# Chunk 0's two norms inside the setup block, a transfer of their own for their modulation rows, and x loaded ahead of W_dt

## The reference, cut to what matters

```python
x = L0_attn_x                                         # 4 x 2048 x 256
mod = (silu(L0_c) @ L0_wmod).reshape(4, 6, 1, -1)     # layer 1 has its own c and wmod
sa, ca, ga, sb, cb, gb = mod[:, 0], ..., mod[:, 5]
ga = (2 * (ga >= 0) - 1) * maximum(abs(ga), 0.25)     # gb too
h = layernorm(x) * (1 + ca) + sa                      # first norm, then modulation
# inside the attention of layer 0:
xn = (h - mean(h)) / sqrt(var(h) + 1e-5) * norm_w + norm_b      # second norm
z, gate = xn @ W_in, silu(xn @ W_gate)
dt = clip(softplus(z @ W_dt + b_dt), 0.001, 1.0)
B, C = z @ W_B, z @ W_C
state = exp(dt * A) * state + dt * B * z              # scan over the tokens, 16 states
y = (sum over the states of state * C) * gate
x = x + ga * (h + y @ W_out)
```

## Time and profile before

| | us |
|---|---|
| median of 3 runs | 3286.13 |
| the three runs | 3277.07, 3286.13, 3286.29 |
| span of the profiled execution | 3287.9 |
| setup block, to DVE's last operation | 44.4 |
| second block's first operation, to chunk 0's first product from `xnl` on PE | 44.9 to 70.1 |
| chunk 0's first POOL product for the scans | 94.6 |
| busy: PE, DVE, ACT, POOL | 88%, 83%, 64%, 59% |

### The profile page before, as it was taken

One profiled execution on the slowest core, in us unless ns is written; L12 is line 12 of the kernel. 1 busy time (PEld: TensorE's weight loads), 2 busy tenths in 40 slices (PEclk: granted clock), 3 DMA queues, 4 the chain that ended last, 5 costly groups with the idle time before them and its releaser, 6 DMA issues.

```text
span 3287.9 us, 45422 instructions
## 1 busy us (share of the span) xinstructions
PE 2907.9 (88%) x14848; PEld 2380.8 (72%) x14848; DVE 2739.3 (83%) x4612; ACT 2096.2 (64%) x3852; POOL 1925.7 (59%) x1541
## 2 busy tenths in 40 slices
PE   6567698998999899898989989899999989998898
PEld 4455477787877778687777868777777877777676
DVE  3777989797998979799898979889897989989541
ACT  2546476676757677675767767576766767575433
POOL 1766667564766757475675756576575647666110
PEclk8558699999999999999999999999999999999998
DMA  4241123231322323232322323232232323223122
GB/s 130 96 159 39 52 81 111 92 102 64 129 82 91 125 78 100 70 118 85 100 103 81 106 79 125 66 106 92 87 109 86 108 76 121 78 71 120 56 103 76
DMA packets 152778, 308.56 MB, mean 94 GB/s; under 512 B 18368, under 2 KB 96984, under 8 KB 135136
## 3 DMA queue, kind: packets, MB, share of 16 engines
q1 hardware_dynamic: 152000, 302.52, 27.6%
q10 hardware_dynamic: 272, 1.57, 0.1%
q0 software_dynamic: 272, 1.57, 0.1%
HBM read 288.27 MB, written 17.35 MB: 93 GB/s over the span
## 4 chain that ended last, share of the span: by engine, by line
PE 48%; DVE 18%; issue 13%; ACT 12%; POOL 5%; DMA 1%; DVEq 0%; SPq 0%; POOLq 0%; ACTq 0%
PE ps_B L1870 11%; PE ps_B L1765 10%; PE ps_A L1765 8%; DVE hs L1527 8%; PE ps_H L1760 7%; DVE acc L1491 5%; PE ps_H L1778 4%; PE ps_B L1760 3%; POOL bu L1100 3%; PE ps_B L1778 3%; PE ps_B L1917 2%; ACT ps_A L1288 2%; DMA bb<-b_rows 1%; DVE hA L1719 1%; ACT acc L1300 1%
## 5 line engine op out<-in xcount | busy, mean ns | idle before, releaser
L1100 POOL TENSOR_TENSOR bu<-z,bb 128x512 f32<-128x512 f32 x1024 | 1294.2, 1290 | 289.9 <-DVE hs L1527 146.7
L1527 DVE TENSOR_TENSOR_SCAN hs<-ps_A,state,bu 128x512 f32<-128x512 f32 x768 | 976.5, 1276 | 21.7 <-ACT ps_A L1288 11.4
L1288 ACT ACTIVATE ps_A<-dt,a_neg 128x512 f32<-128x512 f32 x1024 | 699.3, 686 | 355.7 <-DVE hs L1527 351.5
L1760 PE MATMUL ps_H<-ident,hs 128*128 128x128 f32 x4096 | 652.6, 294 | 195.3 <-DVE acc L1491 123.1
L1760 PEld LDWEIGHTS ps_H<-ident,hs 128*128 128x128 f32 x4096 | 528.3, 151 | 329.2 <-DVE acc L1491 152.0
L1870 PE MATMUL ps_B<-ws_out,hid 128*128 128x256 f32 x2944 | 699.4, 382 | 15.5 <-ACT hid L1437 6.1
L1491 DVE SCALAR_TENSOR_TENSOR acc<-ps_H,ctok,acc 128x512 f32<-128x512 f32 x960 | 700.2, 731 | 8.0 <-PE ps_H L1760 7.1
L1870 PEld LDWEIGHTS ps_B<-ws_out,hid 128*128 128x128 f32 x2944 | 537.0, 191 | 85.1 <-ACT hid L1437 9.9
L1765 PE MATMUL ps_B<-fh,ws_in 128*128 128x512 f32 x1440 | 537.6, 418 | 10.3 <-DVE bl L1680 4.3
L1527 DVE TENSOR_TENSOR_SCAN hs<-ps_A,bu 128x512 f32<-128x512 f32 x256 | 310.9, 1216 | 32.2 <-ACT ps_A L1288 20.0
L1765 PEld LDWEIGHTS ps_B<-fh,ws_in 128*128 128x128 f32 x1440 | 271.0, 188 | 70.5 <-DVE cb L1664 8.1
(11 more groups left out here) (349 smaller groups left out, 4807.7 us busy)
## 6 DMA issues: line engine op xcount, KB each, us to landing
ws_in<-w_split SPq DMA_DIRECT2D x126, 1024.0 KB, 5.4
bb<-b_rows SPq DMA_DIRECT2D x256, 256.0 KB, 3.9
ws_out<-in_L_ffn_V_rwkv SPq DMA_DIRECT2D x64, 512.0 KB, 5.8
ws_out<-in_L_ffn_W SPq DMA_DIRECT2D x32, 512.0 KB, 6.9
xb<-in_L_attn_x SPq DMA_DIRECT2D x16, 512.0 KB, 5.3
n<-in_L_attn_x SPq DMA_DIRECT2D x16, 512.0 KB, 3.9
w_split<-wsp SPq DMA_DIRECT2D x8, 1024.0 KB, 5.6
out<-xb SPq DMA_DIRECT2D x16, 512.0 KB, 3.2
```

What stands on the lines that cost most here:

```text
L1100: pool.tensor_tensor(bu[:, u % 4, :], z[:, d, :], bb[:, s % 2, :], ALU.mult)\
L1288: act.activation(b.t[:, :], dt[:, d, :], ACT.Exp, scale=a_neg[:, d, s:s + 1])\
L1527: dve.tensor_tensor_scan(hs[:, s % 2, d, :], b.t[:, :], bu[:, k % 4, :], state[:, s, d:d + 1] if i % CPB else 0.0, ALU.mult, ALU.add)\
L1760: return pe.transpose(dst, src, ident[:, :])
```

## The change

- `front_norms_act` and `front_norms_pool` are the norms' code of before, now functions that both blocks use. Chunk 0's two norms are written in the setup block, behind what ACT and POOL have there; ACT's Exp of `a_neg` goes ahead of the second norm, POOL's issue of `wm1` ahead of the modulation. The other 15 chunks are as before.
- DVE signals `u_rows_s` when the rows `sA0`, `cA0`, `gA0` stand. SP then stores these three, waits, and broadcasts them as `mod_s`, still in the setup block; the other two rows are stored when `u_rows` comes.
- SP loads chunk 0 of x between W_gate and W_dt rather than behind W_B.

```diff
+                elif (layer, part) == (0, 0):
+                    dve.tensor_copy(goal, ga).then_inc(u_rows_s, 1)
...
                 for n in range(2):
+                    if n == 1:
+                        sp.dma_start(xb[0][:, :, :], x_v[0:1].rearrange("a p t m -> p (a t) m")).then_inc(s_xin.sem, 16)
                     for at, m, src in pieces[n]:
...
-                sp.dma_start(xb[0][:, :, :], x_v[0:1].rearrange("a p t m -> p (a t) m")).then_inc(s_xin.sem, 16)
...
+                front = MOD_PARTS["s"][1] * C
+                sp.wait_ge(u_rows_s, 1)
+                sp.dma_start(mods[:, 0:front], modrow[0][:, 0:front]).then_inc(u_mods, 16)
+                sp.wait_ge(u_mods, 16)
+                load_mod(sp, "s", 0)
                 sp.wait_ge(u_rows, 1)
-                sp.dma_start(mods[:, 0:LAYER_ROWS[0] * C], modrow[0][:, 0:LAYER_ROWS[0] * C]).then_inc(u_mods, 16)
-                sp.wait_ge(u_mods, 16)
+                sp.dma_start(mods[:, front:LAYER_ROWS[0] * C], modrow[0][:, front:LAYER_ROWS[0] * C]).then_inc(u_mods, 16)
+                sp.wait_ge(u_mods, 32)
...
-                pool.wait_ge(u_mm, 3)
-                pool.dma_start(wm[1][:, :, :], kp(w["L1_wmod"])).then_inc(u_wm[1], 16)
+                for name in front_norms_pool(pool, 0):
+                    if name == "h0":
+                        pool.wait_ge(u_mm, 3)
+                        pool.dma_start(wm[1][:, :, :], kp(w["L1_wmod"])).then_inc(u_wm[1], 16)
...
-                act.wait_ge(u_load, n_small)
-                act.activation(a_neg[:, :, :], a_neg[:, :, :], ACT.Exp).then_inc(u_exp, 1)
+                for name in front_norms_act(act, 0):
+                    if name == "sum1":
+                        act.wait_ge(u_load, n_small)
+                        act.activation(a_neg[:, :, :], a_neg[:, :, :], ACT.Exp).then_inc(u_exp, 1)
...
                     yield "mod_s"
-                    if i % CPB == 0:
+                    if i and i % CPB == 0:
```

More of the change, by code:

```diff
@@ L562, in build @@
         u_rows = sem("u_rows")
+        u_rows_s = sem("u_rows_s")
         u_zero = sem("u_zero")
@@ new lines, in apply, with front_norms_act @@
+        def apply(act, dst, src, rs, nb, sig):
+            for t in range(NT):
+                ins = act.activation(dst[:, t, :], src[:, t, :], ACT.Identity, scale=rs[:, t:t + 1], bias=nb[:, t:t + 1])
+            ins.then_inc(sig.sem, 1)
+        def front_norms_act(act, i):
+            x = xb[i % NX]
+            for n, (ready, at) in enumerate(((s_xin, 16), (s_h0, 1))):
+                yield f"sum{n}"
+                if n == 0:
+                    since(act, s_xg, i)
+                act.wait_ge(ready.sem, ready.at(i, at))
+                for t in range(NT):
+                    ins = act.activation(n0[:, t, :], x[:, t, :], ACT.Identity, accum_out=sum_s[:, t:t + 1])
+                ins.then_inc(s_sum.sem, 1)
+                yield f"sq{n}"
+                act.wait_ge(s_nm.sem, s_nm.at(i, n + 1))
+                for t in range(NT):
+                    ins = act.activation(n0[:, t, :], x[:, t, :], ACT.Square, bias=nm_s[:, t:t + 1],
+                                         accum_out=sq_s[:, t:t + 1])
+                ins.then_inc(s_sq.sem, 1)
+                yield f"norm{n}"
+                act.wait_ge(s_rs.sem, s_rs.at(i, n + 1))
+                apply(act, (x, n0)[n], x, rs_s, nb_s, (s_norm, s_n)[n])
@@ new lines, in front_norms_pool @@
+        def front_norms_pool(pool, i):
+            own = Own(pool, o_pool_n, i)
+            x = xb[i % NX]
+            for n in range(2):
+                yield f"mean{n}"
+                pool.wait_ge(s_sum.sem, s_sum.at(i, n + 1))
+                pool.tensor_scalar(nm_s[:, :], sum_s[:, :], -1.0 / C, None, ALU.mult).then_inc(s_nm.sem, 1)
+                yield f"rstd{n}"
+                pool.wait_ge(s_sq.sem, s_sq.at(i, n + 1))
+                own.step(pool.tensor_scalar(rs_s[:, :], sq_s[:, :], 1.0 / C, EPS, ALU.mult, ALU.add))
+                own.step(pool.tensor_tensor(rs_s[:, :], rs_s[:, :], mhalf[:, :], ALU.pow))
+                pool.tensor_tensor(nb_s[:, :], nm_s[:, :], rs_s[:, :], ALU.mult).then_inc(s_rs.sem, 1)
+                if n == 0:
+                    yield "h0"
+                    mod_ready(pool, "s", i)
+                    pool.wait_ge(s_norm.sem, s_norm.at(i, 1))
+                    own.step(pool.tensor_tensor(x[:, :, :], x[:, :, :], per_tile(m_row("cA0")), ALU.mult))
+                    pool.tensor_tensor(x[:, :, :], x[:, :, :], per_tile(m_row("sA0")), ALU.add)\
+                        .then_inc(s_h0.sem, 1)
+            own.end()
@@ L909, in since_x1 @@
                 used(eng, i - 1, "wo1")
[L911 to L920, removed]
         with nc.Block() as block:
@@ L931, in load_b @@
                       .then_inc(s_bb[s % 2].sem, 16)
[L933 to L938, removed]
-                                 mods[b:b + 1, lo * C:hi * C].to_broadcast([P, (hi - lo) * C]))\
-                      .then_inc(s_mod[part].sem, 16)
                 def step(i, name, k):
@@ L1113, in n_stream @@
                 def n_stream(i):
[L1114 removed]
                     x = xb[i % NX]
[L1116 to L1132 removed]
+                    if i:
+                        yield from front_norms_pool(pool, i)
                     yield "gx"
@@ L1206, in _ @@
             def _(act):
[L1207 to L1232 removed]
+                def n_stream(i):
+                    if i:
+                        yield from front_norms_act(act, i)
                     for c in range(KC):
```

75 lines of the change are left out of this document (25 added, 50 removed).

## The result

The changed kernel takes 3292.36 us (median of 13 runs, 3287.04 to 3295.00) against 3285.09 us of the kernel before (median of 13, 3277.07 to 3292.34). The ratio is 1.0020, 95% interval 1.0011 to 1.0028: 3.6 to 9.2 us slower, 6.7 by the means. Timed again in a later set, against 29 runs of the kernel before, the ratio was 1.0014 (1.0006 to 1.0023), 5.2 us by the means. The change does what it says, 21 us of norms leave the second block, and the kernel is slower by a fifth of a per cent or a little less. The prediction had 3288.5, 2.4 us more than before, and called that no measurable change.

A forecast was written before the change was run, and what follows sets the result against it. Norms lead the front, a chain from Ws/W2 loads through layer 1's rows just under them. Block 6.9 later, less 1.8 for loads, less 2.7 slack: +2.4 us, 3286.13 + 2.4 = 3288.5, range 3277 to 3296.

The forecast's parts named there:

- x ahead of W_dt: Setup block: 512 KB more ahead of `norm_b` in SP's queue shift its chain by 1.5 us; early first norm worth nothing.
- The rows' trip: Setup block, rows through DRAM: store 1.9 us and broadcast 4.4 after 32.3, so rows in SBUF at 38.6.
- The rival on `wm1`: Second rival, setup block: rows' store lands only behind `wm1`, broadcast takes 6.8; +8.1 us, 3294.2; 8 in 100.
- To the end of the second norm: Setup block, from POOL's multiply: 12.7 us instead of 13.5, so the second norm ends at 51.3.
- The reading with the Trainium skill: Second norm: two-input VectorE instructions contend with GpSimd reading SBUF, explaining 0.8 us; with another cause the end is 52.1.
- The border: Between setup and second block: 0.5 us, so the second block begins at 51.8 rather than 44.9, 6.9 later.
- The loads: Start of second block: Ws and W2 take 4.4 us instead of 5.8, so PE starts on Ws at 56.2.
- The rest: Second block: 14.6 us from PE's start to DVE's last row operation, 1.6 from `xnl` to PE's product; front 2.4 later.
- nothing takes the norms' place: First rival, second block: 21.6 us of norms go, 6.9 of setup growth comes back; -14.7, 3271.4; 3 in 100.
- the second chain: Start of second block: loads, Ws transposes, layer 1's rows on PE and DVE, then `xnl`; 2.7 us slack under the norms.
- PE at half clock for 17 us: Third rival, first products to end of z: idle PE leaves its clock down; +19 us, 3305; 3 in 100.
- The fall of the median to the low run: Fourth rival, whole kernel: median falls to the run 9.1 us below it; 3277.07 + 2.4 = 3279.5; 18 in 100.

The follow-up runs named there:

- its rows late: Kernel before with only DVE's rows of layer 1 put behind `xnl` (due 5 in place of -27): 0.9999 (0.9991 to 1.0008), -1.2 us.
- x load back: Changed kernel with the load of x at its old place behind W_B: 1.0005 (0.9997 to 1.0014), +2.2 us against the kernel before.
- x alone: Kernel before with only the load of x moved ahead of W_dt: 1.0008 (0.9999 to 1.0017), +2.6 us.
- the four kernels above: Changed kernel (1.0020), and it with x loaded behind W_B (1.0005), `wm1` issued before the rows (1.0016), or all five rows in one store (1.0019).
- the kernel in which the second chain was moved away, all three edits: Changed kernel with Ws/W2 loads, PE's Ws transposes and layer-1 rows in the setup block, DVE's layer-1 rows behind `xnl`: 0.9953, -15.5 us against before.
- all three and x back: Changed kernel with loads and PE's layer-1 work in setup, DVE's rows behind `xnl`, x loaded behind W_B: 0.9947, -17.2 us against before.
- all three and `wm1` early: Changed kernel with loads and PE's layer-1 work in setup, DVE's rows behind `xnl`, `wm1` issued at about 20: 0.9955, -16.0 us against before.

## Why the prediction was right

It was right in its time (3292.36 lies in 3277 to 3296, within 0.3% of before) and in its mechanism: the norms' gain whole, and given back by a block that starts later. The size is less good than that sounds. The front moved by 3.0 us for a forecast of 2.4, but the times differ by 6.7 and 5.2 in the mean, more than twice the forecast, and the range was wide enough to hold that. Step by step, forecast and measured:

1. *x ahead of W_dt.* L786's counterpart at 14.7, measured 14.51: 1.3 us where 1.5 were taken. The eighth row operation ends at 32.78 (32.50 + 0.28) for 32.3, because PE's layer-0 rows took 7.58 where they had taken 6.94; that 0.6 was in no term. It is not the change's doing: in the kernel before with its rows late, whose setup block is untouched, they took 7.58 too. The x load back and x alone show 1.36 us for this step in either direction, and that the early first norm buys nothing.

2. *The rows' trip.* 38.6 forecast, 39.64 measured. This is the term that was mis-sized, twice and in opposite directions: the store took 3.3 instead of 1.9, and the broadcast's landing 3.4 instead of 4.4. That the trip came out within half a microsecond is luck. The rival on `wm1` was partly true: it had `wm1` land at 35.6 (36.1 measured) and the store behind it. What it got wrong is the price. It added the store's whole 1.9 to the landing, while the store's trip runs beside the transfer and only its end waits (broadcast at 36.11, not 37.5), and it gave the broadcast 6.8, which took 3.4. The trip as a whole took 6.8 us for 6.3 (32.81 to 39.64), not 12. The argument against the rival, that 20 KB share sixteen engines with a transfer on another queue, does not hold, and this store has 12 KB, not 20: the four kernels above show that it lands when `wm1` has.

3. *To the end of the second norm.* 12.7 forecast, 39.64 to 52.35 is 12.7. POOL's four short operations took the 1.67 of the first norm again, not 2.50; the window of the changed kernel over the second norm shows DVE with 0.64 us of work in it:

```profile
45.00:51.00 6.00, 0.00 (x0) 0.00 (x0) 0.64 (x4) 3.93 (x16) 1.67 (x4) 0.50 0.00 0
```

The reading with the Trainium skill ("SBUF — State Buffer", section "Who interferes with whom") gave 51.3 from these terms and 52.1 without it. The stretch itself has decided for the shorter one. The kernel before with its rows late shows the cause apart: with DVE's rows taken away and nothing else changed, the four operations took 1.66 us for 2.50. The kernel with x alone ahead agrees with the Trainium skill's condition of two inputs. There two of the four ran, but for 0.09 us, beside DVE operations with one input (L666, L672 and L673) and took 0.23 and 0.20 us, as with DVE idle; the other two ran for the most part beside operations with two inputs (L676, L678 and L679) and took 0.35 and 1.21.

4. *The border.* 0.5 forecast, 0.27 measured (52.35 to 52.62). The second block began at 52.62 for 51.8: the rows were 1.0 late after steps 1 and 2, and 0.2 came back here.

5. *The loads.* 4.4 forecast, 4.3 measured (52.62 to 56.92). The loads moved into the setup block show what their place behind the border costs as a whole: 4.75 us at the first product.

6. *The rest.* 14.6 forecast from PE's start to DVE's last row operation, 14.7 measured (56.92 to 71.66); `xnl` to PE's first product 1.4 for 1.6. The front ended 3.0 us later where 2.4 were forecast.

That DVE's rows, not something else, held `xnl`, was read from 2.7 us of slack in a timeline. It stood the strongest test here: one number in DVE's table, no work removed, gave 6.6 us at the first product in the changed kernel and 0.85 in the kernel before, and the 0.85 has a cause of its own.

**The rivals.** That nothing takes the norms' place was wrong as it stood (-14.7), but its figure is close to that of the kernel in which the second chain was moved away: -15.5. PE at half clock for 17 us did not come: the first products ran at 0.50 and the clock rose some 4 us after the first of them, as in the kernel before, only 3 us later:

```profile
74.00:76.00 2.00, 2.00 (x6) 1.54 (x5) 1.49 (x4) 0.00 (x0) 0.00 (x0) 0.50 0.00 0
76.00:80.00 4.00, 4.00 (x16) 3.17 (x16) 0.43 (x1) 1.95 (x3) 0.00 (x0) 0.85 0.12 39
```

The fall of the median to the low run did not come either. One sum of the chances is off: half of the second rival, the third and the rest are 9 in 100, not 8.

**What stays open.** The profiled executions are 2.7 us apart, the means of the runs 6.7 and 5.2. The second interval (2.0 to 7.6) holds the front's 3.7, the first (3.6 to 9.2) ends above the front's 2.9. The profiled execution of before took longer than that kernel's mean (span 3287.9 and, as in the changed kernel, 1.8 around it: 3289.7, for a mean of 3285), which hides some 4 us in that pair. Between POOL's first product of chunk 1 and the end of the span, single executions take 3015 to 3029 us, and the two of the changed kernel 3025.0 and 3029.2, with the same program. Whether some 2 us more are due to the change, behind the front, no run here decides.

## What to carry to other kernels

Before work is moved ahead of a block's border, list what is issued first behind that border (here two loads) and follow those to the end: a gain on one chain is worth no more than the slack of the chain just under it, less the delay of the border. The chain of waits shows only the longest; the idle time in front of a joining operation (2.71 us at `xnl`) shows how far the next one is below. And where an order is written down as numbers, an order that was free under the old bound (DVE's rows ahead of `xnl`) has to be set anew once the bound has moved.

## What the runs showed of the hardware

**Beside DVE's rows POOL's small operations take longer.** Four of them on 128x4 took 2.50 us, and 1.66 with the rows moved away; on a chain of waits that 0.84 us was found whole at the next engine's first product.

**A small store can wait for a large load of another queue.** From its issue to the next one, 12 KB took 1.6 us with `wm1` landed before (two kernels), and 20 KB, issued as `wm1` landed, 1.9. With the 1.5 MB in flight on POOL's queue 12 KB took 3.1 to 3.3 in eight profiled executions, and in each the next issue came within 0.2 us of `wm1`'s landing. It is not so for any large transfer: with `wm1` issued before the rows, SP's second store (8 KB, issued at 35.73) had landed by 37.3, while the 384 KB broadcast ahead of it on the same queue landed at 38.3.

**PE's clock at the first product.** In the changed kernel PE is idle 7.7 us ahead of it and its products take 0.76 and 0.63 us (granted 0.50, the 1.2 GHz level); with the rows behind `xnl`, and with all three edits, it had been at work until 1.69 us before, and they take 0.47 and 0.4 from the first on (1.00, the 2.4 GHz level). From PE's first product to POOL's first it is 22.5 us in both of these, and 23.9 to 25.2 in the others: some 2 us which a sum of the durations in the kernel before, whose first products run at the lower level, does not contain. The short gap alone does not decide: with all three and x back, and with all three and `wm1` early, the gap was 1.69 too, and the products began at 0.77. Nor does the idle time ahead of `n0`'s transposes order these kernels: it was 1.59 us with all three, and 2.01 and 0.60 in the two that began at 0.77. What decides is not shown.

**Chunk 0 has two lengths.** From POOL's first product to that of chunk 1 it took 168.0 to 168.5 us in six profiled executions (those of before and of the changed kernel among them), and 164.8 to 166.9 in the other eight. The windows of the stretch after the scans, in the kernel before and then in that with x ahead:

```profile
214.60:219.60 5.00, 3.90 (x16) 3.00 (x16) 3.84 (x8) 1.38 (x3) 0.04 (x1) 0.50 1.00 339
219.60:224.60 5.00, 3.88 (x16) 3.02 (x16) 2.86 (x5) 1.85 (x4) 2.32 (x1) 0.50 0.51 211
224.60:229.60 5.00, 4.49 (x14) 3.74 (x15) 0.26 (x1) 0.00 (x0) 0.00 (x0) 0.64 0.92 324
```

```profile
216.20:221.20 5.00, 3.87 (x16) 3.00 (x16) 3.85 (x8) 1.55 (x3) 0.20 (x1) 0.59 0.96 328
221.20:226.20 5.00, 3.18 (x20) 2.53 (x21) 2.71 (x5) 1.69 (x4) 2.16 (x1) 1.00 0.55 216
```

PE had worked with gaps at 0.50 through the scans in both (2.65 and 2.43 us busy in the five before). In the first the clock rises within the third of these windows, in the second within the first, and the chunk is 2.9 us shorter. What picks the one or the other is not shown; that leaves 1 to 4 us of either sign open in any forecast of this kernel that moves its front.
